# Second attention of a recurrent kernel: order of the remainders, of the first group's row loads and of the feed-forward steps between the scores

## The reference

```
xn = layernorm(x)
q, k, v = xn @ Wq.T, xn @ Wk.T, xn @ Wv.T          # 16 heads of 8
scores = q @ k.T / sqrt(8), causal
s = (softmax(scores) @ v) @ Wo.T
quant(z): blocks of 16 along the last dim, scale = max|z| / 6, values rounded to the FP4 grid
h = silu(quant(xn) @ quant(w_gate).T) * (quant(xn) @ quant(w_up).T)     # 352 wide
g = silu(quant(h) @ quant(w_down).T)
x = x + s * g
```

## Time and profile before

| | us |
|---|---|
| median of three runs | 4549.74 |
| lowest and highest | 4549.35, 4549.98 |
| the profiled execution, its own time | 4550.91 |
| its span in the profile | 4548.7 |
| granted TensorE clock, mean of the span | 0.933 of full |
| PE busy | 3722.6 (82%) |
| DVE busy | 2653.2 (58%) |
| ACT busy | 1852.1 (41%) |
| POOL busy | 846.3 (19%) |

### The profile page before, as it was taken

The page is one execution under the profiler, slowest core; times in us unless marked ns, Lnnn a source line. Parts: engine busy times, 40 slices in busy tenths (PEclk is TensorE's granted clock), DMA queues, the critical chain, the costliest instruction groups (busy, mean ns, idle before and its releaser), DMA issues. The chain is left out here.

```text
span 4548.7 us, 57377 instructions
## 1 busy us (share of the span) xinstructions
PE 3722.6 (82%) x20291; PEld 1891.2 (42%) x20291; DVE 2653.2 (58%) x5687; ACT 1852.1 (41%) x3766; POOL 846.3 (19%) x747
## 2 busy tenths in 40 slices
PE   5888888888888788887888888888888878888777
PEld 2344533444344443444434453344434444344434
DVE  5566556564566546665556645656456654566555
ACT  2444344343434434443344433444343343434324
POOL 0033101240012400223002310024001240013313
PEclk9999999998999999998999989999999999999887
DMA  4000010001000011000100001000100001100030
GB/s 143 29 25 5 32 33 29 29 1 37 29 29 29 1 53 36 13 22 21 44 29 19 11 31 35 29 29 1 37 29 29 29 1 45 36 21 22 3 106 20
DMA packets 85634, 136.91 MB, mean 30 GB/s; under 512 B 12092, under 2 KB 60806, under 8 KB 82758
## 3 DMA queue, kind: packets, MB, share of 16 engines
q1 hardware_dynamic: 79422, 124.15, 8.7%
q10 hardware_dynamic: 5898, 8.77, 0.6%
HBM read 103.75 MB, written 28.34 MB: 29 GB/s over the span
## 5 line engine op out<-in xcount | busy, mean ns | idle before, releaser
L716 DVE TENSOR_REDUCE nmax<-banks 128x1 f32<-128x512 f32 (+3 forms) x1216 | 762.0, 658 | 393.8 <-PE banks L547 206.0
L644 ACT ACTIVATE probs<-banks 128x512 f32<-128x512 f32 (+3 forms) x1536 | 670.7, 497 | 522.7 <-PE banks L565 520.6
L93 PE MATMUL banks<-filler,identb 128*128 128x512 bf16 x2472 | 697.9, 412 | 98.2 <-PEq L73 58.6
L547 PE MATMUL banks<-ks,qs 72*128 72x512 bf16 (+3 forms) x1536 | 467.2, 345 | 95.4 <-DVE nmax L716 73.4
L565 PE MATMUL banks<-qs,ks 74*128 74x512 bf16 (+3 forms) x1536 | 459.1, 336 | 63.5 <-ACT probs L644 28.5
L93 PEld LDWEIGHTS banks<-filler,identb 128*128 128x128 bf16 x2472 | 254.7, 105 | 380.8 <-issue 189.5
L682 POOL TENSOR_SCALAR_AFFINE_SELECT probs<-probs 128x512 f32<-128x512 f32 x256 | 187.9, 734 | 1032.9 <-ACT probs L644 1032.9
L609 PE MATMUL banks<-probs,v 128*32 128x512 f32 (+3 forms) x3072 | 332.2, 504 | 52.7 <-POOL probs L682 28.1
L547 PEld LDWEIGHTS banks<-ks,qs 72*128 72x128 bf16 x1536 | 144.3, 101 | 410.4 <-DVE nmax L716 276.9
L333 POOL TENSOR_TENSOR rstd<-var,neghalf 128x4 f32<-128x4 f32 x24 | 24.3, 1011 | 1551.6 <-DVE var L261 1551.6
L1237 ACT ACTIVATE probs<-banks,nm 128x192 f32<-128x192 f32 x512 | 172.9, 421 | 232.7 <-DVE nm L1194 232.7
(11 more groups left out here) (440 smaller groups left out, 6340.8 us busy)
## 6 DMA issues: line engine op xcount, KB each, us to landing
qs<-parts_scratch SPq DMA_DIRECT2D x288, 96.0 KB
ks<-parts_scratch SPq DMA_DIRECT2D x288, 96.0 KB
parts_scratch<-parts SPq DMA_DIRECT2D x48, 384.0 KB, 2.8
shared<-in_w_h SPq DMA_DIRECT2D x17, 1024.0 KB, 7.8
shared<-in_w SPq DMA_DIRECT2D x25, 256.0 KB, 5.4
qs<-max_parts SPq DMA_DIRECT2D x192, 4.0 KB
x<-in_x SPq DMA_DIRECT2D x9, 256.0 KB, 3.0
w_up_s<-in_w_up ACTq DMA_DIRECT2D x1, 2048.0 KB
```

The costliest lines, as they stand in the source:

```text
L93: nc.tensor.matmul(K.ps[:, bank, :], K.identb[:, :], K.filler[:, :], start=True, stop=True)
L547: mm = nc.tensor.matmul(K.ps[:, b, i * keys:(i + 1) * keys], K.qs[0:72, 4 * g + j, t * P:(t + 1) * P], K.ks[0:72, 4 * g + j, 0:keys], star ...
L644: nc.scalar.activation(probs[:, 4 * (q % QUADS) + m % 4, q0:T], K.ps[:, bank("second", m), q0:T], ACT.Exp, scale=scale).then_inc(exped, 1)
L716: nc.vector.tensor_reduce(nmax[:, t, h:h + len(heads)], K.ps[:, n % 2, 0:len(heads) * keys].rearrange("p (j k) -> p j k", k=keys), AX.X, A ...
```

## The change

In the second layer alone:

- VectorE does five quantisation steps, not seven, ahead of the remainders; the remainder of q, one more step, the remainder of k and the copy of v follow, then the third parts. The other steps come after the barrier.
- `prepare` ends with 15 fillers, not 34, and `attention` begins with 24, not 10.
- The first group's three key loads are issued by ScalarE, the three query loads by SyncE (`split_first`).
- The turn of xq is due at step 0, and the four tiles at steps 2, 4, 6 and 8.

In all layers the load of ones is the last of its group, not the first.

```diff
@@ prepare, VectorE
                 if layer == 1:
                     dve.wait_ge(xn_ready, NT)
-                    beside.run(beside.on_vector, -14)
+                    beside.run(beside.on_vector, -16)
...
                 else:
-                    dve.wait_ge(projected, 3)
                     v = K.ps[:, 2, :].rearrange("p (t h d) -> p t h d", t=NT, d=HD)
                     if rms:
+                        dve.wait_ge(projected, 3)
                         for t in range(NT):
...
-                    else:
-                        nc.vector.tensor_copy(K.v32[:, :, :, 0:HD], v)
-                        beside.run(beside.on_vector, -10)
                 for m, b in enumerate((bq, bk)):
                     dve.wait_ge(first, m + 1)
                     nc.vector.scalar_tensor_tensor(rest[:, m, :], K.ps[:, 4 + m, :], 0.0 if b is None else b,
                                                    parts[:, m, 0, :], ALU.add, ALU.subtract).then_inc(left, 1)
+                    if layer == 1 and m == 0:
+                        beside.run(beside.on_vector, -15)
+                if layer == 1:
+                    dve.wait_ge(projected, 3)
+                    nc.vector.tensor_copy(K.v32[:, :, :, 0:HD], v)
@@ prepare, TensorE
                     if not rms:
-                        keep_busy(nc, K, 3, 34)
+                        keep_busy(nc, K, 3, 15)
@@ spread_loads
-def spread_loads(nc, K, sp):
+def spread_loads(nc, K, sp, keys_from=0):
     sp.wait_ge(K.saved, 32)
     for g in range(NG):
         heads = slice(4 * g, 4 * g + 4)
-        part = lambda m: K.parts_d[m].rearrange("i (d h) t -> i d h t", d=HD)[:, :, heads, :]
-        sp.dma_start(K.ks[72:74, heads, :], K.ones_d[:, heads, :]).then_inc(K.spread[g], 16)
+        queries = K.parts_d[0].rearrange("i (d h) t -> i d h t", d=HD)[:, :, heads, :]
         for i in range(3):
             rows = slice(24 * i, 24 * i + 24)
             sp.dma_start(K.qs[rows, heads, :],
-                         part(0)[i].unsqueeze(0).to_broadcast([3, HD, 4, T])).then_inc(K.spread[g], 16)
-            sp.dma_start(K.ks[rows, heads, :], part(1)).then_inc(K.spread[g], 16)
+                         queries[i].unsqueeze(0).to_broadcast([3, HD, 4, T])).then_inc(K.spread[g], 16)
+            if g >= keys_from:
+                spread_keys(nc, K, sp, g, i)
+        sp.dma_start(K.ks[72:74, heads, :], K.ones_d[:, heads, :]).then_inc(K.spread[g], 16)
+
+
+def spread_keys(nc, K, engine, g, i):
+    heads = slice(4 * g, 4 * g + 4)
+    engine.dma_start(K.ks[24 * i:24 * i + 24, heads, :],
+                     K.parts_d[1].rearrange("i (d h) t -> i d h t", d=HD)[:, :, heads, :]).then_inc(K.spread[g], 16)
@@ attention, ScalarE
             def _(act):
+                if split_first:
+                    act.wait_ge(K.saved, 32)
+                    for i in range(3):
+                        spread_keys(nc, K, act, 0, i)
@@ attention, SyncE
-                    spread_loads(nc, K, sp)
+                    spread_loads(nc, K, sp, 1 if split_first else 0)
@@ class Fp4Ffn
-    XQ_STEP = -5
-    UP_STEPS = -4, -3, 3, 7
+    XQ_STEP = 0
+    UP_STEPS = 2, 4, 6, 8
@@ the loop
-                attention(nc, K, True, K.w1_o, beside=ffn, waits_first=10)
+                attention(nc, K, True, K.w1_o, beside=ffn, waits_first=24, split_first=True)
```

More of the change, by code:

```diff
@@ L477, in attention @@
 def attention(nc, K, causal, wo=None, bo=None, combine=True, beside=None, after_store=False,
-              waits_first=0, fetched=False):
+              waits_first=0, fetched=False, split_first=False):
     (scored, reduced, turned, hi_ready, lo_ready, masked, rows, scored2, exped, weighed, oT_ready, oturned, vec,
```

## The result

| | before | after |
|---|---|---|
| median of 14 runs each | 4549.24 us | 4563.58 us |
| ratio, 95% interval | | 1.0036 [1.0028, 1.0045] |
| the profiled execution, its own time | 4550.91 us | 4563.56 us |
| its span | 4548.7 us | 4561.8 us |
| granted clock, mean of the span | 0.933 | 0.927 |

Slower by 0.36%, some 14 to 16 us. The time lies in the range given, but the likeliest case was "no change".

A forecast was written before the change was run, and what follows sets the result against it. It took the chain through each iteration's second attention as bound: -3.16 - 0.31 - 0.5 + 4.65 = +0.68 us, times eight +5.4, less 1.6 in the first attention, +3.8: median 4553.5 us, range 4534 to 4570.

The forecast's parts named there:

- no change: Whole program: median 4553.5 us, +0.08%, not told from an unchanged run; 0.48 for same.
- Part 1, remainders first: VectorE's preparation before the second attention: remainders finish earlier, so row loads start 3.16 us sooner per iteration.
- Part 2: First group's row loads in the second attention: ones last gains 0.31 us, keys on ScalarE's queue 0.5, per iteration.
- a landing under 8 us: First row load to first score: expected about 9 us; under 8 would show the prediction wrong.
- Ones last: First group's loads: moving the ones to the end issues the first query load 0.31 us earlier, all counted as gain.
- The split: Keys on ScalarE's queue, queries on SyncE's: 0.5 us gain per iteration, bounds a 0.3 us loss and 2.2 us gain.
- issue is not what is short: First group's row loads: landing is paced by a backlog behind few DMA engines, so shorter issue gains little.
- Part 3, at full clock: Feed-forward steps between scores: first score to max_parts (the mark) takes 18.6 us against 14.0, costing 4.65 per iteration.
- The first fall of the clock: TensorE's clock halves near the first score in all eight iterations; mean excess up to the mark 2.26 us.
- what comes behind the mark is untouched by the change: Stretch after max_parts, where the second scores' rows are sent: stays as before, 44.7 us in five of eight iterations.
- the slower rival: A second clock fall behind the mark in all eight iterations adds 22 us: 4575; chance 0.15.
- the first attention's 1.6: First attention's row loads: ones last there gains 0.2 us per iteration, 1.6 us in all.

The follow-up runs named there:

- e5: Kernel before with only the change's remainder order and its fillers (15 and 24); loads, ones and steps as before: 4507.8 us, ratio 0.992.
- e3: Changed kernel plus fillers in TensorE's second wait, seven ahead of step 11 and five ahead of the first second score: 4544.4 us, 0.9996 of before.
- e6: Kernel before with only the feed-forward steps moved between the scores (0 and 2, 4, 6, 8): 4607.5 us, ratio 1.0143.
- e1: Changed kernel with the feed-forward steps back where they were (-5 and -4, -3, 3, 7): 4501.4 us, 0.9898 of before.
- e2: Changed kernel with the first group's keys back on SyncE's queue, ones still last: 4574.9 us, 1.0065 of before.
- e4: Changed kernel with 44 fillers instead of 24 ahead of the first score: 4534.4 us, 0.998 of before.
- e8: Changed kernel with 44 fillers ahead of the first score and seven and five in the second wait: 4515.8 us, 0.9942 of before.
- e10: Kernel before with fillers alone in TensorE's standings around the scores; order of remainders, loads and steps as before: 4516.7 us, ratio 0.9946.
- e9: Changed kernel with feed-forward steps back (-5 and -4, -3, 3, 7) and fillers in every TensorE standing around the scores: 4485.4 us, 0.9876 of before.
- e11: Changed kernel, steps at -5 and -4, 1, 3, 7 (one projection ahead of the scores), fillers around the scores: 4490.3 us, 0.9879 of before.

## Why the prediction was right in most of its parts and wrong in its sum

- **Part 1, remainders first.** -3.16 us expected, -3.36 measured. Its value was undersold: alone it takes TensorE's standing from ahead of the first score, and in five of eight iterations the clock holds there. That gain shows alone (e5), and the change throws it away by moving the projections.
- **Part 2.** The prediction named a landing under 8 us as a sign that it is wrong, and the landing is 7.83. Ones last: 0.31 expected, nothing measured (9.25 and 9.22). The split: 0.5 taken from bounds of -0.3 and 2.2, 1.4 measured. The step that failed is "issue is not what is short", read from the earlier trace rows, a window of the last group's backlog; the first group has no backlog ahead of it, and its landing follows its own last issue by 5.1 us. The rule of the Trainium skill (page "DMA: Bandwidth & Descriptors", section "Rules for kernel authors") that several issuing engines only save issue time holds to the letter: 1.32 us of issue saved, 1.4 us of landing. My reading of it as 0 was wrong, because issue lay on the path.
- **Part 3, at full clock.** 18.6 expected, 18.57 measured. The bookkeeping of a projection, its product and the reductions behind it is right. The cost against the old order is 4.6 us in the kernel before, and 4.2 (14.40) where the remainders come first.
- **The first fall of the clock.** In all eight iterations, as expected; excess 2.01 us against 2.26.
- **The step that failed:** "what comes behind the mark is untouched by the change". It went from 45.89 to 47.95 us, because the fall that three iterations of before had behind the mark came in all eight. This was the slower rival, with its mechanism; e3 shows it by removal, e6 by addition. It was given 0.15. The prediction priced such a fall at 3.9 us, from the two longest of the earlier trace rows, 22 us in all; it cost 3.25 over 44.7, which makes 16.5. From 4553.5 these 16.5 make 4570; the landing took 4.9 us less than in the sum, the start 1.6, the first fall 2.0, and the first attention's 1.6 did not come, which gives 4563. That the time lies as near as 10 us to the forecast is in part luck: the other misses together hide 7 of the 16.5 us behind the mark.

Why five of eight iterations of the kernel before escaped that fall is open. Its standings there are as long (1.42 and 1.00 us in the first), only 0.6 us further apart, and no run varied the distance. The windows do show which ones escaped. The five with 44.7 us are those that ran to the mark at the lower clock (0.81 to 0.83); the three with the later fall had 0.89, 0.90 and 1.00. In e1 and e5 all four later falls are in the eight iterations that reached the mark at 1.00, none in the eight that had an early fall. For the interleaved order this doesn't hold: after and e6 have both falls in all eight iterations, e2 in seven, and e4 has the later one without the early one. That the twelve fillers remove the fall is shown; the rest is not.

**Without the clock** the change is worth nothing: its order filled (e8) takes 80.7 us in the stage and 4515.8 in all, the order before filled (e10) 81.3 and 4516.7, ratios that overlap. 5.0 us of earlier scores are paid with 4.6 us between them.

## What to carry to other kernels

Before light work is moved out of a wait for a transfer into a stretch that bounds the stage, ask what else it did in that wait: here the two projections hid behind the landing, and with them there the clock's fall behind the mark came in three of eight iterations instead of all. Moving them cost 62 us in the kernel before. With the standings filled on both sides (e8 against e9) the same move costs 30, 16 of them in the stage. So an order should be compared with TensorE's standings filled too; otherwise a good part (remainders first, -0.8%) and a bad one (+1.4%) can't be told from their sum. A stretch that repeats to 0.1 us in most iterations and is longer in a few can tip over in all of them, and "untouched" is then not a safe assumption for it.

## What the runs showed that was not expected

- **The rest of the loop moves by itself.** Code that stands alike in all these kernels (but for the place of the load of ones) takes between 454.0 and 457.7 us per iteration, up to 30 us over the loop, with clock falls in other places. Single iterations lie further apart: 450.9 us at a granted clock of 0.96 (the second of e5), 460.0 at 0.94 (the seventh of before). e4's gain is mostly this, and e11 loses its lead to it. Which falls come there is not explained by these runs, so differences under some 10 us between two orders are not worth a story.
- **The landing of a group of small transfers followed its last issue** by 5.1 to 5.2 us in the mean with one queue or two (4.8 to 5.8 in single iterations of before), at 0.35 (e2) and 0.36 (after) of sixteen DMA engines busy:

```profile
180.40:188.26 7.86, 3.19 (x15) 1.27 (x13) 4.39 (x8) 0.00 (x0) 0.00 (x0) 0.84 0.36 108
```
